# Layer 0 attention: the value products of four head pairs in one burst of four 32-column groups

## The reference

```python
h = jnp.concatenate([x, latents], axis=1)             # 64 context rows and 256 x rows
q = (latents @ q_w + q_b).reshape(b, k_len, NH, DH)   # 16 heads of 16 features
kv = (h @ kv_w + kv_b).reshape(b, p + k_len, NH, DH, 2)
kmat, v = (kv[..., 0], kv[..., 1])
attn = jnp.einsum('bkhd,bnhd->bhkn', q, kmat) / DH
attn = jnp.where(full_mask[:, None, None, :], attn, -jnp.inf)
attn = jax.nn.softmax(attn.astype(jnp.float32), axis=-1)
attn_out = jnp.einsum('bhkn,bnhd->bkhd', attn, v).reshape(b, k_len, H)
attn_out = attn_out @ out_w + out_b + residual
```

## Time and profile before

| | |
|---|---|
| median of 3 runs | 888.38 us (888.24 to 889.83) |
| the profiled execution's own time | 887.71 us |
| its span, first to last instruction | 886.0 us |
| PE busy | 796.1 us (90%) |
| DVE, ACT, POOL busy | 549.2, 408.1, 365.1 us |
| mean granted TensorE clock | 0.963 |
| V of layer 0 (L610), busy | 83.4 us, 640 instructions |

### The profile page before, as it was taken

How to read it: one execution, slowest core, us unless ns; L and a number is a source line. 1 busy time by engine, 2 the same in 40 slices (tenths; PEclk the granted TensorE clock), 3 DMA queues, 4 the chain that set the end, 5 groups by cost and what they waited for, 6 DMA issues and landing times.

```text
span 886.0 us, 13090 instructions
## 1 busy us (share of the span) xinstructions
PE 796.1 (90%) x4823; PEld 600.9 (68%) x4823; DVE 549.2 (62%) x1090; ACT 408.1 (46%) x965; POOL 365.1 (41%) x384
## 2 busy tenths in 40 slices
PE   3899999999579978869999999999998989876898
PEld 3788887887459745447775677777566769544598
DVE  3665756666583289965745756444579466379644
ACT  1676675867332257744452222554223231266431
POOL 3465453546520358854312663000466512257300
PEclk8999999999979989999999999999999989997799
DMA  7300000000000500001432000223000000200001
GB/s 187 129 2 1 1 1 1 2 1 1 1 1 1 188 2 1 1 1 48 149 137 95 1 1 1 95 97 95 1 1 0 1 1 1 95 1 1 1 13 37
DMA packets 24003, 30.87 MB, mean 35 GB/s; under 512 B 3628, under 2 KB 16772, under 8 KB 23940
## 3 DMA queue, kind: packets, MB, share of 16 engines
q1 hardware_dynamic: 23400, 30.03, 10.4%
q10 hardware_dynamic: 540, 0.01, 0.0%
HBM read 28.98 MB, written 1.05 MB: 34 GB/s over the span
## 4 chain that ended last, share of the span: by engine, by line
PE 70%; DVE 14%; issue 6%; POOL 5%; ACT 3%; ACTq 1%; DMA 1%; POOLq 0%; DVEq 0%
PE wide_ps L439 8%; PE narrow_ps L458 7%; PE narrow_ps L610 7%; PE wide_ps L757 7%; PE wide_ps L486 6%; PE wide_ps L710 5%; PE narrow_ps L792 5%; PE wide_ps L744 3%; PE wide_ps L731 3%; DVE scoresb L1229 2%; DVE mx L1238 2%; PE wide_ps L712 2%; PE wide_ps L419 2%; DVE sums L1245 2%; POOL probs L1521 2%
## 5 line engine op out<-in xcount | busy, mean ns | idle before, releaser
L914 ACT ACTIVATE probsT<-wide_ps 128x640 f32<-128x640 f32 (+1 forms) x104 | 86.1, 828 | 139.0 <-PE wide_ps L486 138.2
L1513 POOL TENSOR_TENSOR scoresb<-scoresb,mx 128x768 f32<-128x768 f32 (+1 forms) x40 | 70.7, 1768 | 167.9 <-DVE mx L1236 129.3
L1533 POOL TENSOR_TENSOR probs<-scoresb,rcp 128x512 f32<-128x512 f32 (+1 forms) x128 | 91.4, 737 | 77.6 <-DVE rcp L1313 77.6
L486 PE MATMUL wide_ps<-ident,probs 128*128 128x128 f32 x640 | 91.8, 282 | 29.0 <-POOL probs L1521 23.6
L486 PEld LDWEIGHTS wide_ps<-ident,probs 128*128 128x128 f32 x640 | 74.4, 145 | 56.4 <-issue 54.7
L1499 POOL TENSOR_TENSOR rstd<-veps,mhalf 128x1 f32<-128x1 f32 x56 | 32.1, 573 | 149.3 <-DVE veps L1164 149.3
L610 PE MATMUL narrow_ps<-probsT,vpad 128*64 128x128 f32 x640 | 83.4, 278 | 1.4 <-ACT xq L914 1.4
L1521 POOL TENSOR_TENSOR probs<-scoresb,rcp 128x1024 f32<-128x1024 f32 x40 | 78.9, 1972 | 8.3 <-DVE rcp L1246 8.3
L610 PEld LDWEIGHTS narrow_ps<-probsT,vpad 128*64 128x64 f32 x640 | 68.2, 136 | 13.8 <-issue 11.1
L439 PE MATMUL wide_ps<-xq_r,wstream_r 128*128 128x512 f32 x192 | 65.3, 424 | 8.5 <-issue 6.8
L458 PEld LDWEIGHTS narrow_ps<-wstream_r,hidden 128*128 128x128 f32 x576 | 69.1, 188 | 1.2 <-DVE xB L1192 0.5
(11 more groups left out here) (170 smaller groups left out, 1643.0 us busy)
## 6 DMA issues: line engine op xcount, KB each, us to landing
wstream<-in_L_xattn_wq SPq DMA_DIRECT2D x8, 512.0 KB, 3.9
wstream<-in_L_xattn_wk SPq DMA_DIRECT2D x8, 512.0 KB, 4.9
wstream<-in_L_xattn_wv SPq DMA_DIRECT2D x8, 512.0 KB, 5.8
wstream<-in_L_xattn_wo SPq DMA_DIRECT2D x8, 512.0 KB, 7.6
wstream<-in_L_xattn_mlp_w SPq DMA_DIRECT2D x2, 1024.0 KB, 6.1
wstream<-in_L_xattn_w_fc SPq DMA_DIRECT2D x2, 1024.0 KB, 7.6
xq<-in_x SPq DMA_DIRECT2D x1, 1024.0 KB, 5.6
wstream<-in_L_xattn_fc_w SPq DMA_DIRECT2D x1, 1024.0 KB, 4.8
```

Source lines behind the costliest of these rows:

```text
L486: m = nc.tensor.transpose(ps[:, j * P:(j + 1) * P], probs[:, u % 2, j * P:(j + 1) * P], ident[:])
L914: nc.scalar.activation(dst, src, ACT.Identity, **kw).then_inc(ring.drained[ring.slot(key)], 1)
L1513: g.tensor_tensor(s3[:, first:], s3[:, first:], mx[:, u % 3, first:].unsqueeze(2).broadcast_to([P, 16 - first, n_scores]), ALU.subtract).t ...
L1533: g.tensor_tensor(probs[:, u % 2, o:o + 2 * n].rearrange("p (i k) -> p i k", i=2), s3[:, :, lo:hi], rcp[:, u % 3, 0:2].unsqueeze(2).broadc ...
```

## The change

`units0` walks four head pairs for one query half, then the same four for the other half, then the next four. V is issued for a group of four units at a time, in step 4, 8, 12, ...: 20 matmuls, each with a stationary tile of 32 columns, the four units of the group as neighbours in the order and each in its own 32-row group of the narrow slot. The count of matmuls stays at 320 (640 instructions); their stationary tile is 32 instead of 64 columns. Since four units must be kept, the copies of T go to six buffers (`turned_probs`) instead of two.

The values of the context rows (`vctx`) of all four batches are computed at the start, in two jobs, and not by batch; `v` is one job now instead of two. `kpair` is copied in six pieces instead of five, cut at 1280 so that heads of the two groups do not share a piece; the last piece of a batch is made in that batch's own first step. `SIDE0` and `START0` are put in a new order: ahead of the first scores there are two more jobs.

```diff
-        units0 = [(b, r, q) for b in range(B) for r in range(H0 // 2) for q in range(2)]
+        units0 = [(b, 4 * c + j, q) for b in range(B) for c in range(NC) for q in range(2) for j in range(4)]
...
-        SIDE0 = [("q",), ("proj", 0), ("proj", 1), ("k", 0), ("k", 1), ("qhot", 0), ("qhot", 1), ("kpair", 0),
-                 ("kpair", 1), ("qhot", 2), ("kpair", 2), ("kpair", 3), ("qhot", 3), ("kpair", 4), ("v", 0), ("v", 1)]
-
-        START0 = [[("q",), ("k", 0), ("qhot", 0), ("kpair", 0), ("kpair", 1)],
-                  [("v", 0), ("v", 1), ("k", 1), ("qhot", 1), ("kpair", 2), ("kpair", 3), ("qhot", 2), ("qhot", 3),
-                   ("kpair", 4)]]
+        SIDE0 = [("kpair", 5), ("proj", 0), ("proj", 1), ("q",), ("k", 0), ("k", 1), ("qhot", 0), ("kpair", 0),
+                 ("kpair", 1), ("qhot", 1), ("kpair", 2), ("v",), ("qhot", 2), ("kpair", 3), ("qhot", 3), ("kpair", 4)]
+        PIECES = [(0, 512), (512, 1024), (1024, 1280), (1280, 1792), (1792, 2304), (2304, 2560)]
+
+        START0 = [[("q",), ("k", 0), ("qhot", 0), ("kpair", 0), ("kpair", 1), ("qhot", 1), ("kpair", 2)],
+                  [("v",), ("vctx", 0), ("vctx", 1), ("k", 1), ("qhot", 2), ("kpair", 3), ("kpair", 4), ("qhot", 3),
+                   ("kpair", 5)]]
...
+            if s == 0:
+                return (job, b) if 0 < b < B else (None, None)
...
+        TURNED0 = 6
+
+        def turned_probs(u):
+
+            if u >= len(units0):
+                return probsT[:, u % 2, :]
+            i = u % TURNED0
+            flat = probsT[:].rearrange("p a n -> p (a n)")
+            return flat[:, i * 640:(i + 1) * 640] if i < 3 else turned_mem[:, (i - 3) * 640:(i - 2) * 640]
...
+                elif kind == "vctx":
+
+                    ps, filled = take_narrow((job, b), 4, among)
+                    pe.wait_ge(ctxd_ready, 1)
+                    for i in range(2):
+                        for kc in range(NC):
+                            m = mm(ps[:, i * D:(i + 1) * D], ctxD[:, kc, 2 * job[1] + i, :, :].rearrange("p a k -> p (a k)"),
+                                   kv_w0[:, kc, 1, :], start=kc == 0, stop=kc == NC - 1)
...
-                for j in range(5):
-                    i, kb = j // 2, j % 2
-                    lhs = (vp[:, (kb * 16 + 2 * r + i) * 64:(kb * 16 + 2 * r + i + 1) * 64] if j < 4 else
-                           vp[:, 2048 + r * 64:2048 + (r + 1) * 64])
-                    po = 64 * (r % 4 // 2)
-                    m = mm(ps[po:po + 64, qoff(q)], lhs, probsT[:, u % 2, j * P:(j + 1) * P],
-                           start=(r % 2, q, j) == (0, 0, 0), stop=(r % 2, q, j) == (1, 1, 4))
-                if r % 4 == 3 and q == 1:
+                for k in range(5):
+                    i, kb = k // 2, k % 2
+                    for j in range(4):
+                        r = 4 * c + j
+                        h = 2 * r + i
+                        lhs = (vpad0[b % 2][:, kb * 512 + h * 32:kb * 512 + (h + 1) * 32] if k < 4 else
+                               vctx0[b][:, r * 32:(r + 1) * 32])
+                        m = mm(ps[32 * j:32 * j + 32, qoff(q)], lhs, turned_probs(4 * group + j)[:, k * P:(k + 1) * P],
+                               start=k == 0, stop=k == 4)
+                if q == 1:
                     m.then_inc(filled, 1)
...
-                if 0 <= step - 1 < n0:
-                    values0(step - 1)
+                if step > 0 and step % 4 == 0:
+                    values0(step // 4 - 1)
```

More of the change, by code:

```diff
@@ L569, in side_product0 @@
                     ps, filled = take_narrow((job, b), 1, among)
-                    lo, hi = 512 * job[1], 512 * (job[1] + 1)
+                    lo, hi = PIECES[job[1]]
                     for r in range(lo // KEYS0, -(-hi // KEYS0)):
@@ L584, in scores0 @@
                     pe.wait_ge(*narrow.empty((("qhot", r // 2), b)))
-                    for piece in range(r * KEYS0 // 512, -(-(r + 1) * KEYS0 // 512)):
-                        pe.wait_ge(*narrow.empty((("kpair", piece), b)))
+                    for piece, (lo, hi) in enumerate(PIECES):
+                        if lo < (r + 1) * KEYS0 and hi > r * KEYS0:
+                            pe.wait_ge(*narrow.empty((("kpair", piece), b)))
                 for i in range(2):
@@ L957, in probs_turned @@
                 n = 5 if u < len(units0) else 8
-                evac(probsT[:, u % 2, 0:n * P], wide_ps[:, wide.slot(key), 0:n * P], wide, key)
+                evac(turned_probs(u)[:, 0:n * P], wide_ps[:, wide.slot(key), 0:n * P], wide, key)
             def side0_copy(job, b):
                 key = (job, b)
-                if job[0] in ("proj", "v"):
+                if job[0] in ("proj", "v", "vctx"):
                     return
@@ L969, in side0_copy @@
                 if job[0] == "kpair":
-                    evac(kpair[:].rearrange("p r k -> p (r k)")[:, 512 * job[1]:512 * (job[1] + 1)], ps, narrow, key)
+                    lo, hi = PIECES[job[1]]
+                    evac(kpair[:].rearrange("p r k -> p (r k)")[:, lo:hi], ps[:, 0:hi - lo], narrow, key)
                 elif job[0] == "qhot":
@@ L1553, in _ @@
                           ).then_inc(ctxd_ready, 1)
[L1554 to L1555 removed]
+            for lo, hi in ((0, 2048), (2048, 3072)):
+                g.memset(vpad_mem[:, lo:hi], 0.0).then_inc(vzero, 1)
             pool.wait_ge(load["rows"], 16 * len(ROWS))
```

58 lines of the change are left out of this document (27 added, 31 removed).

## The result

The changed kernel takes 881.73 us (median of 5 runs, 880.17 to 883.22) against 888.79 for the kernel before in the same comparison: ratio 0.9906, 95% interval 0.9885 to 0.9926. So it is faster, by some 8 us. The forecast was 17.4: right in direction, and too large by about 9 us.

The account below looks back on a forecast made before the run. Layer 0 was taken as bound by PE, in program order. Gains of 5.9, 13.0 and 1.2 us in the batches, less 2.7 at the start, made 17.4: 870.3 on the profiled execution, 871 as median, range 860 to 885.

Parts of the forecast that it names:

- V, 1.17 us a group: Layer 0: a group of 40 V instructions takes 1.17 us, at 0.025 an instruction against 0.107 before.
- The circle, 2.17 us a unit: Layer 0: dependences over two units, T through ACT, DVE and POOL to T again, pace plain steps at 2.17 us.
- PE time in a plain step is worth 0.06 us: Steps without a side job: removing PE time gains only 0.06 us, from 2.23 down to 2.17.
- The norm, 9.44: Steps 1 to 3 of a batch, T(49) to T(52): 9.44 us in place of 10.67.
- Batches 0 to 2, 41.7 and 45.0: Layer 0: batch 0 falls from 47.6 to 41.7 us, batches 1 and 2 from 51.5 to 45.0 each.
- the 42.5 of the sum without collisions: Batches 1 and 2: step lengths sum to 41.8 us, plus 0.7 for MLP weight preparation on ACT and DVE.
- collisions: One engine's late step meeting another's long one: 2.5 us a batch taken, between 0 and 4 possible.
- The start, 2.7: Before the first scores: the added jobs make T(0) 2.7 us later; bounds 1.5 and 5.
- Batch 3, 36.0: T(48) to T(63), the batch that prepares nothing: 36.0 us instead of 37.2, a gain of 1.2.
- My argument against it: Against a low clock in layer 0: a half-speed PE is always busy, and in layer 3 the clock came back.
- my rival: Layer 0's clock falls to 1.2 GHz; change turns slower at about 50 us of it, 907 us possible; chance 0.12.
- Behind T(63), "nothing changes": After layer 0's last transposes T(63): the rest stays as before, the last V ending within 0.2 us.

Follow-up runs that it names:

- e4_serial: Changed kernel with each V group's products issued one unit after another, so neighbours share a 32-row group; 916.26 us, ratio 1.0299.
- e2_split: Changed kernel with layer 0's first four transposes of each T waiting only for the first half of the unit's probabilities; 873.92 us, ratio 0.9823.
- e10_bsplit: Kernel before the change, with only the split wait for the first four transposes of each T; 888.61 us against 890.94, ratio 0.9971.
- e3_start: Changed kernel with both `vctx` jobs moved from the start into batch 0's steps 1 and 2, last `kpair` piece into step 0; 877.29 us.
- e1_fill: Changed kernel with unread filler matmuls on TensorE in nine light steps of batch 3; 873.48 us, ratio 0.9825.
- c1_after: The changed kernel run once more, unedited, beside the follow-up runs; 880.67 us, ratio 0.9903 to the kernel before.
- e11_fill_tail: Changed kernel with unread filler matmuls only in steps 57, 58, 59, 61 and 62 of batch 3; 876.1 us, ratio 0.9823.
- e12_stall_only: Changed kernel with the score products of units 53 and 54 issued four times, during batch 3's norm waits; 879.11 us, ratio 0.9865.
- e9_fill_start: Changed kernel with batch 3 filler and the context-value jobs moved off the start, without the split wait; 870.13 us, ratio 0.9765.
- e7_best: Changed kernel with batch 3 filler, the split wait of T and the context-value jobs moved off the start; 869.61 us, ratio 0.9768.
- e5_vshort: Changed kernel with V making only the first of five products of each unit, attended values incomplete; 874.55 us, ratio 0.9838.

## Why the prediction was right or wrong

*V, 1.17 us a group: right.* 1.23 to 1.28 at the full clock, and the row groups do overlap (`e4_serial`, 0.12 an instruction where they don't).

*The circle, 2.17 us a unit: right.* 4.32 to 4.34 for two units in batch 3, released by POOL, and `e2_split` moves it to 3.97. The sentence that PE time in a plain step is worth 0.06 us holds before the change (`e10_bsplit`) and explains why the change gains only where side jobs stand.

*The norm, 9.44: too short by 0.5.* 9.95 in batches 2 and 3 of the profiled execution. In its batch 1 it took 10.61, with the clock at 0.60 from 92 to 96 us.

*Batches 0 to 2, 41.7 and 45.0: right*, 42.0 and 44.0 to 46.7. At the full clock a batch takes 44.04, which is 1.5 above the 42.5 of the sum without collisions: 0.5 for the norm and 1.0 for collisions, not 2.5. Batch 1 shows the clock instead, 0.93 and 46.65. That 45.0 is as near as it is to both executions is in part luck, since collisions put too high stood in for a clock put at nothing.

*The start, 2.7: right on average* (3.0), 4.0 in the profiled execution.

*Batch 3, 36.0: wrong, by 4.9 us.* The step that failed is the clock, which the sum puts at nothing. I gave it a chance of 0.12 and looked for it in long stretches at the low level, priced by the side-job unit; where it matters most there are no side jobs. My argument against it was that a PE at half speed is busy all the time. In this kernel it isn't, for the norm waits and the circle set the pace: in batch 3 PE is busy for 28.27 of 40.87 us, and from 184 to 188 us for 1.44 of 4.00. From 40 to 200 us some 26 us ran at the low level (clock 0.91, 0.91, 1.00 and 0.85 in four pieces of 40 us; a piece at 0.91 holds 2 x 0.09 x 40 = 7.2 us of it), against none before. It is not the 50 us of my rival, but the circle passes the low clock on: a T of 1.30 or a V of 2.29 us lies on the path.

The rows are batch 3, T(48) to T(63), in the changed kernel, in `e3_start`, in `e1_fill` and in `e2_split`, in the columns of the earlier trace rows:

```profile
174.00:214.87 40.87, 28.27 (x271) 21.49 (x272) 22.86 (x68) 26.64 (x78) 22.03 (x32) 0.83 0.00 1
```

```profile
170.24:208.84 38.60, 25.32 (x272) 19.17 (x272) 22.97 (x68) 26.71 (x78) 21.99 (x32) 0.90 0.00 1
```

```profile
172.68:209.08 36.40, 29.99 (x308) 23.33 (x308) 23.46 (x68) 26.71 (x78) 21.99 (x32) 1.00 0.01 2
```

```profile
170.34:207.09 36.75, 25.56 (x274) 19.28 (x273) 23.11 (x68) 26.73 (x79) 21.86 (x33) 0.90 0.00 1
```

Set in order, batch 3 follows its clock:

| batch 3 | granted clock | us |
|---|---|---|
| changed kernel | 0.83 | 40.87 |
| `c1_after` | 0.82 | 40.67 |
| `e3_start` | 0.90 | 38.60 |
| `e11_fill_tail` | 0.91 | 38.58 |
| `e12_stall_only` | 0.94 | 37.08 |
| `e1_fill` | 1.00 | 36.40 |
| `e9_fill_start` | 1.00 | 36.42 |
| `e2_split` (split) | 0.90 | 36.75 |
| `e7_best` (split) | 1.00 | 35.17 |

ACT, DVE and POOL are busy as long in all of them, within 0.7 us. So of the 4.9 us the clock has 4.5 (40.87 less 36.40), and the 0.4 left is about what the norm took too long. `e3_start` has the same program in batch 3 as the changed kernel and was 2 us faster there: how much of a stretch runs at the low level can differ where the program does not.

*Behind T(63), "nothing changes": wrong, by 4.0 to 5.5 us.* The failed step is the same one. Since the clock is low behind T(63), the projections take 2.04 instead of 1.1 us, and POOL's multiplications start 13.2 and 14.3 us behind T(63) instead of 9.5; from there on the exit is as long as before. Over all profiles: where the clock stays at 1.00 from T(63) to POOL's first multiplication (the two with the order of before and full V, and the five filled to the end) POOL starts 9.3 to 9.5 us behind T(63) and the exit is 40.5 to 41.1 us; in the eight others the clock is low on that way, POOL starts after 11.9 to 14.5 and the exit is 43.6 to 45.5 (in `e4_serial` the longer last burst of V counts too). `e11_fill_tail` shows that the clock at the exit is enough to undo the loss (41.0). That is not all: of the 4.6 us that the fill takes back at the exit, kernels with a short exit keep 2.0 at the end (mean T(63) to the end 664.5 us over the five of them, 666.5 over the seven others in the new order; the kernel before has 660.9, `e10_bsplit` 662.0). The layers behind have clock falls of their own, which come or stay away. The three rows are the same piece of layer 1, 20 to 30 us behind its first `q`, in the profiled execution of the changed kernel, in `c1_after` and in the kernel before:

```profile
313.60:323.60 10.00, 7.05 (x48) 4.15 (x48) 9.31 (x14) 6.99 (x22) 8.50 (x6) 1.00 0.00 0
```

```profile
309.00:319.00 10.00, 7.27 (x40) 4.60 (x40) 8.61 (x13) 6.46 (x22) 8.42 (x6) 0.83 0.00 0
```

```profile
319.20:329.20 10.00, 7.27 (x40) 4.62 (x40) 8.61 (x13) 6.45 (x22) 8.40 (x6) 0.83 0.00 0
```

Two executions of the same kernel differ here, and the whole way from the first `q` to layer 2 takes 171.3 us in the one and 172.9 in the other (173.0 before, 174.3 to 176.5 in the five kernels that are filled to the end of batch 3, but also 174.3 in three that are not: `e2_split`, `e4_serial` and `e5_vshort`). Why the kernels with the fill lose there stays open; no run was made for it.

The sum closes for the profiled execution: start 1.3, batches 0.3, 1.7 and -1.0, batch 3 4.9, behind it 5.5, together 12.7, which is 883.0 less the forecast's 870.3.
